# Value blocks of every second pair of images: three scaled ScalarE copies in place of one masked VectorE product

## What is computed

```python
qkv = (x @ w_qkv).reshape(B, N, 3, H, Dh)
q, k, v = (qkv[0], qkv[1], qkv[2])            # after a transpose to heads first
attn = ...                                    # softmax over keys, softmax over queries, or a polynomial
out = jnp.einsum('bhnm,bhmd->bhnd', attn, v)
out = jnp.transpose(out, (0, 2, 1, 3)).reshape(B, N, C)
return out @ w_proj + b_proj
```

## Time and profile before

| what | us |
|---|---|
| three runs | 499.46, 507.44, 508.05 (median 507.44) |
| profiled execution, its own time | 501.84 |
| span of that execution, first to last instruction | 500.1 |
| TensorE busy in it | 460.0 (92%) |
| VectorE busy | 260.1 (52%) |
| ScalarE busy | 174.7 (35%) |
| GpSimd busy | 88.9 (18%) |
| granted TensorE clock, mean | 0.971 of full speed |

### The profile page before, as it was taken

How to read it: one execution, slowest core, us unless ns; L and a number is a source line. 1 busy time by engine, 2 the same in 40 slices (tenths; PEclk the granted TensorE clock), 3 DMA queues, 4 the chain that set the end, 5 groups by cost and what they waited for, 6 DMA issues and landing times.

```text
span 500.1 us, 9635 instructions
## 1 busy us (share of the span) xinstructions
PE 460.0 (92%) x3788; PEld 396.2 (79%) x3788; DVE 260.1 (52%) x714; ACT 174.7 (35%) x427; POOL 88.9 (18%) x154
## 2 busy tenths in 40 slices
PE   4799999989999998999999998899999999999990
PEld 4766776878887887887765878788998989999990
DVE  4287744654658476563553546786567632212212
ACT  0332243133341462726273441375312103343340
POOL 2022100002121202002200002420012137722211
PEclk9999989999999999999999999999999589999996
DMA  8950000000030000000000720015621002898603
GB/s 302 239 129 1 1 2 0 1 2 1 1 93 1 1 1 2 2 1 1 0 1 0 225 62 1 1 55 157 223 77 35 6 26 61 277 295 274 202 2 109
DMA packets 14820, 35.93 MB, mean 72 GB/s; under 512 B 2719, under 2 KB 8223, under 8 KB 14582
## 3 DMA queue, kind: packets, MB, share of 16 engines
q1 hardware_dynamic: 12424, 31.42, 20.9%
q0 software_dynamic: 1632, 2.59, 1.7%
q10 hardware_dynamic: 720, 1.32, 0.7%
HBM read 32.49 MB, written 3.59 MB: 72 GB/s over the span
## 4 chain that ended last, share of the span: by engine, by line
PE 80%; DVE 11%; ACT 3%; issue 3%; DMA 2%; POOL 0%; SPq 0%; POOLq 0%; DVEq 0%; ACTq 0%
PE bank L1435 11%; PE bank L1382 9%; PE bank L1473 7%; PE bank L1415 6%; PE bank L1657 6%; PE bank L1459 5%; PE bank L1749 4%; PE bank L1703 4%; PE bank L1718 3%; PE bank L1463 3%; PE bank L1690 3%; PE bank L1488 3%; PE bank L1424 2%; PE bank L1673 2%; PE bank L1396 1%
## 5 line engine op out<-in xcount | busy, mean ns | idle before, releaser
L574 POOL TENSOR_TENSOR rstd<-rstd_tmp,minus_half 111x3 f32<-111x3 f32 x20 | 17.2, 858 | 294.0 <-DVE rstd_tmp L899 294.0
L1382 PE MATMUL bank<-constants 128*128 128x128 f32 x514 | 67.4, 288 | 0.0
L1382 PEld LDWEIGHTS bank<-constants 128*128 128x128 f32 x514 | 63.8, 201 | 2.3 <-issue 1.4
L1435 PE MATMUL bank<-arena 96*111 96x192 f32 (+1 forms) x320 | 56.8, 327 | 0.0
L1435 PEld LDWEIGHTS bank<-arena 96*111 96x111 f32 (+1 forms) x320 | 52.1, 175 | 2.2 <-issue 2.1
L1415 PE MATMUL bank<-nT,arena 96*96 96x296 f32 (+1 forms) x144 | 39.7, 420 | 0.8 <-DVE nT L914 0.8
L1473 PE MATMUL bank<-arena,et 128*128 128x192 f32 x204 | 37.4, 334 | 0.0
L704 ACT ACTIVATE xn<-h,minus_mean_rstd,rstd 111x192 f32<-111x192 f32 (+1 forms) x48 | 22.6, 536 | 37.9 <-POOL minus_mean_rstd L581 37.9
L936 DVE TENSOR_TENSOR vblk<-bank,constants 111x384 f32<-111x384 f32 x40 | 21.8, 555 | 26.1 <-PE bank L1435 17.9
L1473 PEld LDWEIGHTS bank<-arena,et 128*128 128x128 f32 x204 | 32.7, 190 | 1.9
L1657 PE MATMUL bank<-arena,qT 96*64 96x222 f32 (+1 forms) x320 | 32.4, 354 | 1.0 <-DVE arena L927 0.7
(11 more groups left out here) (263 smaller groups left out, 782.0 us busy)
## 6 DMA issues: line engine op xcount, KB each, us to landing
arena<-in_w SPq DMA_DIRECT2D x17, 576.0 KB, 5.6
arena<-in_w SPq DMA_DIRECT2D x17, 384.0 KB, 3.7
arena<-in_w SPq DMA_DIRECT2D x34, 96.0 KB, 4.1
arena<-in_patches SPq DMA_DIRECT2D x4, 606.0 KB, 7.8
arena<-in_c SPq DMA_DIRECT2D x2, 576.0 KB, 10.5
arena<-in_wpack SPq DMA_DIRECT2D x2, 576.0 KB
arena<-in_wpack SPq DMA_DIRECT2D x1, 1152.0 KB
arena<-in_wpack SPq DMA_DIRECT2D x1, 1008.0 KB
```

The lines of the kernel that those rows point to most:

```text
L1382: mm(PS[b][:, 0:128], ident, ident, start=True, stop=True)
L1435: last = mm(o, nrep[q][k][0:96 + k, im], w(n + "_qkv", k, 2 * D, D), start=(k == 0), stop=(k == 1 and n != "B"))
```

## The change

In each W phase VectorE keeps the pairs at places 0 and 2 of the four, and ScalarE takes those at places 1 and 3. For each of its pairs ScalarE waits for the bank and then issues three copies out of it, one for each row group's head r: 111 rows x 8 groups x 16 columns, multiplied by a per-row scale that is one column of `mask_v` (1 in row group r, 0 elsewhere). The third copy releases the bank. There are 5 layers x 2 halves x 2 pairs = 20 such pairs: 20 VectorE products go, 60 ScalarE copies come. On ScalarE they stand at the place of the W phase, behind the S phase's work and ahead of everything of the later phases. TensorE's program, GpSimd's and all DMAs are as before.

```diff
@@ ScalarE's program
+            def value_blocks(n, p):
+
+                j = ("v", n, p)
+                act.wait_ge(*filled(j))
+                src = bank(j)[0:GR, 0:2 * D].rearrange("p (a r e) -> p a r e", r=HG, e=HD)
+                dst = vblk[:, 2 * p:2 * p + 2].rearrange("p i g r e -> p (i g) r e")
+                for r in range(HG):
+                    ins = sc.activation(dst[:, :, r, 0:HD], src[:, :, r], ACT.Copy, scale=con("mask_v", GR)[:, HD * r:HD * r + 1])
+                    if r < HG - 1:
+                        mark(ins)
+                ins.then_inc(*freed(j))
@@
+                if ph == "W":
+                    for p in ps[1::2]:
+                        value_blocks(n, p)
@@ VectorE's program
                 if ph == "W":
-                    for p in ps:
+                    for p in ps[::2]:
                         value_blocks(n, p)
```

## The result

The changed kernel takes 535.61 us (median of 6 runs, 529.37 to 537.21) against 503.59 us (median of 6 runs, 498.88 to 508.05): 1.067 times the time, 95% interval 1.062 to 1.072 (the ratio on record is formed from part of the executions; that of the two medians is 1.064). The forecast was slower, 518 us with a range of 509 to 529; the loss, 32 us, is more than twice the 12.9 us of the sum.

The account below looks back on a forecast made before the run. TensorE was taken to bound the kernel, with VectorE's relief worth nothing. Stalls of 7.05 + 3.5 + 1.7 + 0.5 + 0.1 = 12.9 us on a mean of 505.0 gave 518 us (chance 0.62), range 509 to 529.

Parts of the forecast that it names:

- What bounds the kernel: TensorE, busy 460.0 us, 92% of the span; nobody waits for the value product, so freeing VectorE's 11.1 us gains nothing.
- The price of a pair: On ScalarE, three copies out of PSUM per pair: 0.376 + 2 x 0.257 = 0.89 us.
- The rival prices, 0.56 and 1.15: Bounds per pair on ScalarE: 0.56 us, the one product replaced; 1.15 us, three scaled activations of 192 columns.
- The 22.6 us for all sixty copies: ScalarE time added by the copies, 60 x 0.376 us, twice what VectorE gives up.
- What is held up: Behind six of ten W phases ScalarE's normalisation runs late and TensorE waits; the other four cost 0.1 us together.
- E.W1: W phase where late rows, partly covered by the transposes of E.X1, delay E.O1 from 306.50 to 307.03: 0.5 us.
- The sum of the stalls: TensorE's added waits, 7.05 + 3.5 + 1.7 + 0.5 + 0.1 = 12.9 us, all reaching the end.
- rival (2): Part is given back at TensorE's existing waits: 3 to 5 us of 12.9 vanish, 514 us; chance 0.16.
- rival (3): Not slower: VectorE time is on the path after all; 493.9 us if all 11.1 us counted; chance 0.03.
- rival (1): The stalls also cost granted clock: five drops of 1.6 us, 8.0 us on top, up to 526 us; chance 0.19.
- the stretch 320 to 324: Kernel before: TensorE busy 1.99 of 4.00 us kept clock 1.00; a 2.35 us stall leaves about as little.
- the price of a fall: Clock loss per drop, from the stretch 68 to 72 at 0.60 on average: 4 x 0.4 = 1.6 us.

Follow-up runs that it names:

- e6: The change made only in the four W phases behind which ScalarE has no normalisation, the other six as before; mean 504.6 us, 1.000 to before.
- e1: The changed kernel, but ScalarE takes the pairs at places 0 and 1 of each W phase, VectorE those at 2 and 3; 503.9 us, 0.999 to before.
- e9: The changed kernel with dummy matmuls filling its six stalls to size and 26 existing TensorE gaps; mean 512.5 us, 1.020 to before.
- e8: The kernel before, with dummy matmuls in 26 idle times of TensorE of 0.3 to 1.4 us; mean 498.8 us, 0.996 to before.
- e3: The kernel before, with ScalarE only waiting in each W phase until the last value bank is full, copying nothing; mean 516.7 us, 1.028 to before.
- e11: The change made only in C.W1, the phase with the longest stall, the rest as before; mean 513.1 us, 1.024 to before.
- e5: The changed kernel with dummy matmuls sized to fill its six stalls, the wait kept; mean 521.7 us, 1.036 to before.
- e10: The kernel before with 26 gaps filled by dummy matmuls and 7 more ahead of A.T0; mean 496.4 us, 0.989 to before.

## Why the prediction was wrong

**What bounds the kernel.** Right. Nobody waited for the value product, and taking half of them (in e6 a fifth) from VectorE gained nothing that shows: e1 and e6 are at 0.999 and 1.000, each with an interval of 0.006 to either side.

**The price of a pair.** Right: 0.89 us expected, 0.89 measured. The estimate from the figures of the Trainium skill ("ScalarE: Activation LUTs", section "What ACT_TABLE_LOAD costs"), 0.97 us, is a little high: one copy took 371 ns in the median where it gives 386. The rival prices, 0.56 and 1.15, can be dropped. The 22.6 us for all sixty copies was wrong, and at odds with the price of a pair: neighbours overlap, so twenty pairs are 20 x 0.89 = 17.8 us, and 17.7 were measured. Nothing in the sum rests on it.

**What is held up.** Right in all six places, and right about the four others. The idle times at the transposes: 2.3, 2.3, 3.5, 1.7 and 2.3 us forecast; 2.27, 2.27, 3.45, 1.66 and 2.27 measured. At E.W1 the size was off: 0.5 us was forecast and the delay there grew by 1.2 (0.72 at the transposes, and VectorE's steps for F.T0 moved the output of E.O1 with them).

**The sum of the stalls.** 12.9 us forecast; 13.7 us in the profiled pair, 13.7 and 14.7 between e9 and e8, 12.4 to 14.4 by span times clock. Of that almost nothing was given back (0.5 us ahead of C.O1, inside a stretch at the lower clock), so rival (2) falls; so does rival (3).

**The step that failed** is the clock, rival (1). It was named, and given 0.19 instead of most of the chance, and its price was also too small at a place. Two readings led there. First, the stretch 320 to 324, half idle at a clock of 1.00, was taken to show that a stall of 2.3 us is harmless. One stretch of one execution shows only that it can be. In the kernel after the same stretch of the program had the clock down (the row of 334.12 to 357.00, 0.78), and two stalls of 2.27 us were followed by a fall while one wasn't. Second, the price of a fall was read from the one at 68 to 72 as 1.6 us; in the profiled execution behind the three stalls that were followed by one it cost 3.4 each, and in the stretch with its own gaps 5.0. In the mean of the executions the time at the lower level rose by 37.6 us, which costs up to 18.8 us. With that, which only the runs after gave, the forecast would have been 503 + 13 + 17 to 19, or 533 to 535 us. The rule of the Trainium skill that stood beside the rival ("TensorE: Matmul & The Clock Gate", section "HAM oscillation — how this bites in real kernels"), that gaps bring the clock down again each time, pointed the right way. The trace agrees in part: the waits that the Trainium skill describes there, about 3 to 5 us, are longer than five of the six stalls here, and not each of the stalls did it.

The spread of the three runs of before, 8.6 us, was in front of the reader too. It was used to place the forecast, and not asked for its cause. That cause is the granted clock: over 41 executions of an unchanged kernel the time at the lower level goes from 20 to 40 us at an almost constant span times clock. A kernel that is already at the lower level for 30 us, by different amounts each time, is one in which a new stall may well cost clock; that is argued, not tested.

What stays open is which stalls bring the clock down. C.T0 and E.T1 did with 2.27 us and C.T1 did not in the same execution; in e3 C.T1 did with 1.51 and C.T0 did not; C.W1 alone cost 9.9 us in the mean in e11, of which its profiled execution shows 8.1 at that place, against 6.4 between the two profiled executions of before and after. No run varied the length of a single stall alone, and each kernel has one profiled execution.

## What to carry to other kernels

Work given to an idle engine is paid by what stands behind it in that engine's order: look for the latest wait that the new work brings, and for the next thing on the same engine that the bound engine needs. Here taking the pairs at places 0 and 1 instead of 1 and 3, or issuing the normalisation first, made the same move free. Count a stall of TensorE at two to two and a half times its length (27.5 us for 13.7 in the profiled pair, 31.2 for 12.4 in the means) while the clock is not proven to stay up, and divide each execution into span times clock and the rest before comparing.

## What the runs showed of the hardware that was not expected

The cost of a stall in TensorE was more in the clock than in the stall: 18.8 us beside 12.4 by the measure over all executions, or 31.2 - 14.7 = 16.5 us if the stalls are taken from e9. Dummy matmuls in a stall whose length they don't change brought back 12.7 us (e5), and 138 dummy instructions in gaps of 0.3 to 1.9 us made the kernel before faster by 1.1% (e10) with the time at the lower level cut from 30.6 to 15.5 us. In the kernel before 21 of these 27 gaps lie in layers B to G, where the profiled execution had a granted clock of 1.00 throughout; only the mean of many executions shows that they cost something.
